# Warp products on finished byte addresses, loaded sixteen at a time; router gates from one tanh

## The reference

```python
# stage 0, cond: rigid transform of each image, bilinear from four neighbours
ix = (gx_n + 1.0) * 0.5 * (w - 1);  iy = (gy_n + 1.0) * 0.5 * (h - 1)
ix0, iy0 = floor(ix), floor(iy);    wx1, wy1 = ix - ix0, iy - iy0
out = gather(iy0i, ix0i) * (wy0 * wx0) + gather(iy0i, ix1i) * (wy0 * wx1)
    + gather(iy1i, ix0i) * (wy1 * wx0) + gather(iy1i, ix1i) * (wy1 * wx1)
# stage 0, ffn: two ternary linear layers with a gelu between (act_quant, weight_quant)
# stage 1, cond: attention pooling within an image (tanh scores, mask, softmax)
# stage 1, ffn: four experts, the best two per row
logits = xf @ wr + br
topk_vals, topk_idx = jax.lax.top_k(logits, 2)
gates = jax.nn.softmax(topk_vals, axis=-1)
out = einsum('nk,nkd->nd', gates, y_sel - c_sel + c_sum)
# stage 2: an adapter with a layer norm, then a frequency-domain product
# stage 3: a linear layer chosen by category, then a gated ternary ffn with a silu
```

## Time and profile before

| | |
|---|---|
| time, 3 runs | 2594.36 us median, 2581.16 to 2600.14 |
| the profiled execution | 2577.68 us, span 2575.9 us |
| granted TensorE clock, mean | 0.912 |
| DVE instructions in the profile | 7954, of them 4096 warp products |

### The profile page before, as it was taken

How to read it: one execution, slowest core, us unless ns; L and a number is a source line. 1 busy time by engine, 2 the same in 40 slices (tenths; PEclk the granted TensorE clock), 3 DMA queues, 4 the chain that set the end, 5 groups by cost and what they waited for, 6 DMA issues and landing times. The chain is left out here.

```text
span 2575.9 us, 50738 instructions
## 1 busy us (share of the span) xinstructions
PE 2090.7 (81%) x12000; PEld 1613.5 (63%) x12000; DVE 1786.6 (69%) x7954; ACT 1647.6 (64%) x2802; POOL 988.1 (38%) x1092
## 2 busy tenths in 40 slices
PE   1334697888888898898898889988888898999975
PEld 1112476666766676676676667766766777777742
DVE  4878777677777777777787778777877564544344
ACT  1035556566777776776777778777666587767542
POOL 1434455545444544344444444454434211221110
PEclk8655799999999999998999999999999999999977
DMA  7344544354545545534455455554554445355531
GB/s 256 110 143 129 170 118 144 112 154 127 149 124 166 150 150 146 175 114 131 141 176 156 137 151 156 169 172 146 142 173 142 125 141 165 122 169 178 158 97 53
DMA packets 306147, 375.94 MB, mean 146 GB/s; under 512 B 127122, under 2 KB 251447, under 8 KB 292924
## 3 DMA queue, kind: packets, MB, share of 16 engines
q1 hardware_dynamic: 274848, 297.02, 37.9%
q0 software_dynamic: 28672, 68.21, 9.4%
q10 hardware_dynamic: 2332, 7.47, 0.7%
HBM read 291.23 MB, written 72.93 MB: 141 GB/s over the span
## 5 line engine op out<-in xcount | busy, mean ns | idle before, releaser
L1177 POOL DMA_INDIRECT w_win<-in_windows,w_idx x512 | 524.0, 1024 | 831.7 <-DMA w_win<-in_windows,w_idx 645.4
L799 DVE TENSOR_TENSOR w_prod<-w_win,w_hat 128x36 f32<-128x36 f32 x4096 | 530.4, 220 | 266.0 <-issue 263.2
L1568 PE MATMUL bank<-moe_w,moe_hidden_T 128*128 x2528 | 644.1, 396 | 18.0 <-DVE moe_y L1010 11.2
L1552 PE MATMUL bank<-moe_xT,moe_w_tile 128*128 128x256 f32 (+1 forms) x3008 | 636.4, 356 | 8.1 <-ACT moe_xT L1337 7.7
L1552 PEld LDWEIGHTS bank<-moe_xT,moe_w_tile 128*128 128x128 f32 x3008 | 513.2, 195 | 84.0 <-ACT moe_xT L1337 14.7
L1568 PEld LDWEIGHTS bank<-moe_w,moe_hidden_T 128*128 128x128 f32 x2528 | 474.5, 197 | 98.2 <-issue 36.5
L1354 ACT ACTIVATE moe_hidden_T<-bank,moe_b 128x256 f32<-128x256 f32 (+1 forms) x752 | 288.6, 436 | 166.0 <-PE bank L1552 139.5
L1354 ACT ACT_TABLE_LOAD x151 | 193.7, 1283 | 71.6 <-PE bank L1552 55.4
L1211 POOL DMA_INDIRECT moe_y_back<-moe_out_sorted,rows_back x128 | 127.7, 998 | 275.6 <-DMA moe_y_back<-moe_out_sorted,rows_back 152.7
L1197 POOL DMA_INDIRECT moe_in_sorted<-c,rows x128 | 138.3, 1080 | 245.1 <-DVE rows L940 104.3
L1096 DVE SCALAR_TENSOR_TENSOR hidden_back<-bank,back_stats,hidden_back 128x512 f32<-128x512 f32 x128 | 95.3, 745 | 107.4 <-ACT hidden_back L1394 105.6
(11 more groups left out here) (260 smaller groups left out, 3749.2 us busy)
## 6 DMA issues: line engine op xcount, KB each, us to landing
moe_w_tile<-in_moe_w SPq DMA_DIRECT2D x94, 1024.0 KB
L_cond_W<-in_L_cond_W SPq DMA_DIRECT2D x128, 256.0 KB
adapters<-in_adapter SPq DMA_DIRECT2D x128, 192.5 KB
gamma_beta<-in_gamma_beta SPq DMA_DIRECT2D x128, 128.0 KB
moe_x<-moe_in_sorted SPq DMA_DIRECT2D x64, 256.0 KB
moe_out_sorted<-moe_y SPq DMA_DIRECT2D x64, 256.0 KB
x_front<-in_x SPq DMA_DIRECT2D x32, 256.0 KB
w_win<-in_windows,w_idx POOLq DMA_INDIRECT x512
```

Source lines behind the costliest of these rows:

```text
L799: ins = v.tensor_tensor(out3, win, hy, ALU.mult)
L1177: gp.indirect_dma_start(out=V[:, g_ * WLEN:(g_ + 1) * WLEN], out_offset=None, in_=t["windows"], in_offset=bass.IndirectOffsetOnAxis(ap=idx ...
L1552: last = te.matmul((H0, H1)[r % 2][:, (f % FPU) * TILE:(f % FPU) * TILE + width(n)], W1[n % 3][:, d * F + f * P:d * F + (f + 1) * P], XT[: ...
L1568: last = te.matmul(Y[:, u * D:(u + 1) * D], hT[:, (f % (2 * FPU)) * TILE + u * P:(f % (2 * FPU)) * TILE + (u + 1) * P], ap(moe2, weight + ...
```

## The change

1. V is allocated first, at the fixed byte address V_AT = 16512 of each partition. `prepare` turns the table of element offsets into finished byte addresses: times 4, plus V_AT, plus the image's place in V (a new column W_AT of the constants). One more small DVE instruction, once.
2. A product's window is given by the register alone, as an access of bytes cast to float32. The register arithmetic per product (multiply, add) has nothing left to compute.
3. The 32 registers of an image are loaded sixteen at a time. The load for k = 0 to 15 is issued in the previous image, directly behind L803's add and ahead of the yield; the load for k = 16 to 31 stands between the second and third batch of products, ahead of the yield there. The wait for a group's offsets (`s_off`) moves with the first load to the end of the previous group.
4. Router: ACT takes Tanh (scale 0.5) instead of Exp; DVE multiplies it by the mask of the second choice (OH + 8) instead of by the mask of both, sums, and two TENSOR_SCALARs on 128x2 write the gates 0.5 - 0.5 s and 0.5 + 0.5 s. The reciprocal, two products and one reduction are gone. Three bare yields keep the places in the order.

```diff
-            ch.link(v.scalar_tensor_tensor(woff[:, :], low[:, 0:PX], float(WY), low[:, PX:2 * PX], ALU.mult, ALU.add))
+            ch.link(v.scalar_tensor_tensor(low[:, 0:PX], low[:, 0:PX], float(WY), low[:, PX:2 * PX], ALU.mult, ALU.add))
+            ch.link(v.tensor_scalar(woff[:, :], low[:, 0:PX], 4.0, wcst[:, W_AT:W_AT + 1], ALU.mult, ALU.add))
...
+            V8 = V.bitcast(U8)
+            def addresses(q, a, j_):
+                par, low_ = q % 2, V_AT + 4 * a * IWIN
+                if a == 0 and j_ == 0:
+                    dve.wait_ge(s_off[par], 8 * (q - par) + 16)
+                first = woff[par][0:1, a * PX + j_ * GI:a * PX + (j_ + 2) * GI]
+                _, at = nc.values_load_multi_w_load_instructions(
+                    first, engines=[mybir.EngineType.DVE], min_val=low_, max_val=low_ + 4 * ((WX - TAP) * WY + WY - TAP),
...
+                return [r.with_bounds(guaranteed_mod_val=0, out_of_modulus=4) - V_AT for r in at]
+            def window(at):
+                return bass.AP(tensor=V8, offset=at, ap=[[4 * QI * IWIN, P], [4 * WLEN, NG], [4 * WY, TAP], [1, 4 * TAP]]).bitcast(F32)
...
+                    if q == 0 and a == 0:
+                        ready[:] = addresses(q, a, 0)
                     dve.wait_ge(s_win[a], 16 * NG * (q + 1))
-                    if a == 0:
-                        dve.wait_ge(s_off[par], 8 * (q - par) + 16)
...
-                    first = woff[par][0:1, a * PX:(a + 1) * PX]
-                    _, shift = nc.values_load_multi_w_load_instructions(
...
                         if k and k % GI == 0:
+                            if k % (2 * GI) == 0:
+                                ready[:] = addresses(q, a, k // GI)
                             yield
-                        win = ap(V, shift[k] + a * IWIN, [[WLEN, NG], [WY, TAP], [1, TAP]])
+                        win = window(ready[k % (2 * GI)])
...
-                    yield from ch.spaced(v.tensor_tensor(col, row(0), row(1), ALU.add))
+                    add = v.tensor_tensor(col, row(0), row(1), ALU.add)
+                    add.then_inc(ch.sem, 1)
...
+                    if a + 1 < QI or q + 1 < NQ:
+                        ready[:] = addresses(q + (a + 1) // QI, (a + 1) % QI, 0)
+                    yield
+                    dve.wait_ge(ch.sem, step)
...
-                ins = v.tensor_tensor(lg[:, EX:EX + 8], lg[:, EX:EX + 8], lg[:, SL:SL + 8], ALU.mult)
+                ins = v.tensor_tensor(lg[:, EX:EX + 8], lg[:, EX:EX + 8], lg[:, OH + 8:OH + 16], ALU.mult)
...
-                yield from ch.spaced(v.reciprocal(lg[:, SE:SE + TT], lg[:, SE:SE + TT]))
-                ins = v.tensor_tensor(ap(lg, GA, [[EXP, TT], [1, EXP]]), e3, ap(lg, SE, [[1, TT], [0, EXP]]), ALU.mult)
-                yield from ch.spaced(ins)
+                g0 = q * 2 * TT
+                v.tensor_scalar(GP[:, g0:g0 + TT], lg[:, SE:SE + TT], -0.5, 0.5, ALU.mult, ALU.add)
+                v.tensor_scalar(GP[:, g0 + TT:g0 + 2 * TT], lg[:, SE:SE + TT], 0.5, 0.5, ALU.mult,
+                                ALU.add).then_inc(E["m_gat"], 1)
...
-                yield from ch.spaced(v.tensor_tensor(prod, slot2, both(GA), ALU.mult))
-                v.tensor_reduce(GP[:, bass.ds(q * 2 * TT, 2 * TT)], ap(lg, PR, [[EXP, 2 * TT], [1, EXP]]), AX.X,
-                                ALU.add).then_inc(E["m_gat"], 1)
+                yield
+                yield
+                yield
...
-                s.activation(lg[:, 82:90], lg[:, 0:8], ACT.Exp).then_inc(E["a_lge"], 1)
+                s.activation(lg[:, 82:90], lg[:, 0:8], ACT.Tanh, scale=0.5).then_inc(E["a_lge"], 1)
```

More of the change, by code:

```diff
@@ L15 @@
 I32 = mybir.dt.int32
+U8 = mybir.dt.uint8
 ALU = mybir.AluOpType
@@ L75 @@
 WLEN = WX * WY
+V_AT = 16512
 MKW = P + 1
@@ L79 @@
 QPX = QI * IPX
-W_GX, W_GY, W_IV, W_JV, W_BASE = 0, NG, NG + 1, NG + 1 + GI, NG + 1 + GI + GJ
+W_GX, W_GY, W_IV, W_JV, W_AT, W_BASE = 0, NG, NG + 1, NG + 1 + GI, NG + 1 + GI + GJ, NG + 2 + GI + GJ
 WCONST = W_BASE + B
@@ L257, in sem @@
             return ctx.enter_context(nc.semaphore(name))
+        V = sb("w_win", QI * IWIN)
         cst = sb("const", CCONST)
@@ L432, in _ @@
             ch.link(v.tensor_scalar(low[:, :], low[:, :], MAGIC, 0.0, ALU.subtract, ALU.max))
-            v.tensor_tensor(fd[:, :], fd[:, :], low[:, :], ALU.subtract)
-            ch.link(v.scalar_tensor_tensor(woff[:, :], low[:, 0:PX], float(WY), low[:, PX:2 * PX], ALU.mult, ALU.add))
+            ch.link(v.tensor_tensor(fd[:, :], fd[:, :], low[:, :], ALU.subtract))
+            ch.link(v.scalar_tensor_tensor(low[:, 0:PX], low[:, 0:PX], float(WY), low[:, PX:2 * PX], ALU.mult, ALU.add))
+            ch.link(v.tensor_scalar(woff[:, :], low[:, 0:PX], 4.0, wcst[:, W_AT:W_AT + 1], ALU.mult, ALU.add))
             dve.sem_inc(s_geo, 1)
@@ L440, in network @@
         ("cst", "idb", "wq", "wmean", "moe2", "moeb1", "router", "brB"))
-    b1B, b2B, fbB, attW, attb, attv, freqM, KB, ones, ids, nhalf, hmag, frD, fdD, idxD, offD, XS, YS, XMD = (g[k] for k in
+    b1B, b2B, fbB, attW, attb, attv, freqM, KB, ones, ids, nhalf, hmag, frD, fdD, idxD, offD, XS, YS, XMD, V = (g[k] for k in
         ("b1B", "b2B", "fbB", "attW", "attb", "attv", "freqM", "KB", "ones", "ids", "nhalf", "hmag", "frD", "fdD", "idxD",
-         "offD", "XS", "YS", "XMD"))
+         "offD", "XS", "YS", "XMD", "V"))
     s_raw, s_ld = g["s_raw"], g["s_ld"]
@@ L777, in coords @@
                 ins.then_inc(E["t"], 1)
+            V8 = V.bitcast(U8)
[6 more added lines that the diff above has]
+                    first, engines=[mybir.EngineType.DVE], min_val=low_, max_val=low_ + 4 * ((WX - TAP) * WY + WY - TAP),
+                    skip_runtime_bounds_check_because="the shift inside a group is bounded by its shape for any angle")
+                return [r.with_bounds(guaranteed_mod_val=0, out_of_modulus=4) - V_AT for r in at]
+            def window(at):
+                return bass.AP(tensor=V8, offset=at, ap=[[4 * QI * IWIN, P], [4 * WLEN, NG], [4 * WY, TAP], [1, 4 * TAP]]).bitcast(F32)
+            ready = []
             def warp(q):
@@ L783, in warp @@
                     yield
+                    if q == 0 and a == 0:
+                        ready[:] = addresses(q, a, 0)
                     dve.wait_ge(s_win[a], 16 * NG * (q + 1))
-                    if a == 0:
-                        dve.wait_ge(s_off[par], 8 * (q - par) + 16)
                     if a % 2 == 0:
                         dve.wait_ge(E["hat"], 2 * q + a // 2 + 1)
-                    first = woff[par][0:1, a * PX:(a + 1) * PX]
-                    _, shift = nc.values_load_multi_w_load_instructions(
-                        first, engines=[mybir.EngineType.DVE], min_val=0, max_val=(WX - TAP) * WY + WY - TAP,
-                        skip_runtime_bounds_check_because="the shift inside a group is bounded by its shape for any angle")
                     for k in range(PX):
                         if k and k % GI == 0:
+                            if k % (2 * GI) == 0:
+                                ready[:] = addresses(q, a, k // GI)
                             yield
-                        win = ap(V, shift[k] + a * IWIN, [[WLEN, NG], [WY, TAP], [1, TAP]])
+                        win = window(ready[k % (2 * GI)])
                         hy = ap(H, HY + (a * PX + k) * NG, [[1, NG], [0, TAP], [QPX, TAP]])
@@ L802, in warp @@
                     row = lambda k: ap(M, k * IPX * TAP, [[IPX, TAP], [1, IPX]])
-                    yield from ch.spaced(v.tensor_tensor(col, row(0), row(1), ALU.add))
+                    add = v.tensor_tensor(col, row(0), row(1), ALU.add)
+                    add.then_inc(ch.sem, 1)
+                    ch.n += 1
+                    step = ch.base + ch.n
+                    if a + 1 < QI or q + 1 < NQ:
+                        ready[:] = addresses(q + (a + 1) // QI, (a + 1) % QI, 0)
+                    yield
+                    dve.wait_ge(ch.sem, step)
                     yield from ch.spaced(v.tensor_tensor(col, col, row(2), ALU.add))
@@ L1740 @@
     wc[:, W_JV:W_JV + GJ] = np.arange(GJ)
+    wc[:, W_AT] = V_AT + 4 * IWIN * (p % QI)
     wc[:, W_BASE:] = (np.arange(B)[None, :] * PYW - YLO) * PXR - XLO
```

1 line of the change is left out of this document (removed).

## The result

| | before | after |
|---|---|---|
| time, 20 runs each | 2584.85 us median | 2575.47 us median |
| the profiled execution | 2577.68 us, span 2575.9 | 2571.66 us, span 2569.9 |

The ratio is 0.9953 (95% interval 0.9937 to 0.9970): 12 us less, where the prediction had 71.

What follows compares the result with a forecast made beforehand. DVE was taken to bound the first 2022 us, PE close behind. Savings of 40 + 40 + 5 = 85 us on DVE, 0.8 of them arriving (68), plus 3 from ACT gave 71 us less: 2523 us, range 2462 to 2577.

Steps and rivals of the forecast that it cites:

- A load of 16 values: 1.18 us: DVE's register load: 16 values cost 1.18 us, on a straight line between one value (0.310) and 32 (2.105).
- register operations pace half of the batches: DVE's products: the sequencer paces some batches at 130 ns a product; without register operations all run at 107, 40 us less.
- Idle of 0.73 and 0.80 us behind the two loads: DVE per image: the first load leaves 0.73 us idle, the second 0.80; with 0.11 for a break, 1.64 against 1.95.
- the lead that eight products can win (0.27 us): Before the second load: eight products without register operations win DVE's sequencer 0.27 us of lead over the engine.
- rival 1: More gain: the sequencer is nearly always ahead, loads hide, DVE gains some 185 us, 130 arrive, about 2465 us; chance 0.13.
- The term "40 us" for the load: DVE's register loads: splitting and placing them saves 0.31 us an image, 40 us over 128 images.
- Router 5 us on DVE, 3 us at the end: Router: two fewer small DVE instructions per group save 5 us; ACT's saved table loads count 3 us at the end.
- 0.8 of DVE's gain reaches the end: Whole kernel: 0.8 of the 85 us saved on DVE, 68 us, shortens the total time.
- DVE's busy time, issue and waits for POOL together as 95%: Between 300 and 2000 us: 1307 + 207 + 96 = 1610 of 1700 us, leaving DVE's queue almost no slack.
- POOL as running ahead of DVE: Between 300 and 2000 us: POOL waits 71 us for DVE to give the window back, so it runs ahead.
- rival 2: Gain absorbed: DVE waits for POOL, whose fixed part is above 80%; two thirds of 85 us go, about 2570; chance 0.12.
- Wrong if DVE's waits for POOL grow by more than some 20 us: Sign in the changed kernel's profile: growth of DVE's waits for POOL beyond some 20 us would show the forecast wrong.

Runs made afterwards that it cites:

- e16: Changed kernel with gathers not waiting for each other and register arithmetic kept on every product, fourth chip: 0.9976 of the kernel before.
- e18: Kernel before with the router's tanh change alone, gathers still waiting, fourth chip: 0.9999 of the kernel before.
- e8: Changed kernel with gathers not waiting for each other, but one load of 32 addresses at the image's head: 0.9401 of the kernel before.
- e7: Changed kernel with gathers not waiting for each other, plus an unused 1.21 us DVE reduction per image: 0.9502 of the kernel before.

## Why the prediction was wrong

- *A load of 16 values: 1.18 us.* 1.10, right; so was the reading that register operations pace half of the batches (495 us, as forecast; 477 of 512 batches of eight now take under 1 us, where 259 did).
- *Idle of 0.73 and 0.80 us behind the two loads.* Wrong: inside the loads DVE idles 0.35 and 0.02 us. I gave the sequencer the lead that eight products can win (0.27 us) and no more, and held against rival 1 that the waits before every batch and add take the lead away. Without its register operations it keeps a lead over other threads' instructions too, ten instructions or 1.2 us at the most; with them it has 0.56 us of idle in the same place (e16). The term "40 us" for the load, over the whole span, measured 167 us (225 to 58). That was the mechanism of rival 1, which I gave 0.13.
- *Router 5 us on DVE, 3 us at the end.* The counts are right (26 reloads fewer at the gelus, 32 at the router); at the end nothing that e18 can see.
- *0.8 of DVE's gain reaches the end.* This is the step that decided, and it failed. With a larger gain than forecast (167 us in loads and 35 in products over the whole span, against 80) the time fell by 12, 0.06 of it. I took DVE's busy time, issue and waits for POOL together as 95% and called the bound DVE; the 96 us of waits for POOL belonged to the other side, and they grew by 98 us. And I read POOL as running ahead of DVE from its 71 us of waits for the window, without adding up the rest of its queue, which comes to 91% of the stretch in its own pace. I had 514 and 74 us of landing waits in front of me and left out 61 us of further landing waits and 120 us of issue in the same queue; so I wrote "above 80%" under rival 2.
- *Rival 2, at 2570 us with a chance of 0.12,* is what happened, for its reason. That its number fits is luck: it lets two thirds of 85 us go, where over nine tenths of 202 us went.
- *Wrong if DVE's waits for POOL grow by more than some 20 us.* They grew by 98.

What stays open: the measured slopes don't add up to the result. At 0.15 to 0.36 per microsecond of DVE, 202 us would be 30 to 73 us and not 12. Idle time inside a load may be worth less than engine work (0.17 from e8 to e1, where e7 has 0.36 for work in the same kernel), perhaps because a good part of it would have been a wait for another engine anyway; no run separates that.

## What to carry to other kernels

Before costing a gain on one engine, add up each other engine's queue in the same stretch as busy + waits for its own DMAs + issue. Here the queue that reached 91% that way held the kernel back although its busy share was 46%, and the waits of DVE for its results grew by 98 us, over half of what DVE saved in the stretch. A queue of indirect DMAs that wait for each other's landing is worth a try: here freeing it was worth 7% together with this change on a chip where the change alone gave 0.5%, 3% on another, and nothing there without the change. And compare versions on one chip, side by side: the same edit gave 0.954 and 1.004 on two.

## What the runs showed of the hardware

- A register load takes 0.31 us for one value, 1.10 us for 16 and 2.10 us for 32: 53 ns per value up to 16, 63 ns from 16 to 32.
- DVE's sequencer got up to ten instructions ahead, 6.5 started in the mean during a 1.10 us load between batches, and the load cost the engine 0.02 us. With a 57 ns register operation per product (e16) 3.5 started, and it cost 0.56 us.
- An indirect DMA costs POOL 1.25 us in its queue if it waits for nothing. If it waits for the landing of the one before, it starts 3.5 us behind it (median of after, 2.8 to 5.6 for eight in ten).
- In traces from two of the four chips short sequencer instructions take 0.4 to 1.4 us in places. On the fourth a kernel with free gathers takes 115 to 142 us more than on the first, the kernel before 11.
- None of the router's 32 Tanh had a table load in front of it; the last table loaded before it was in 27 of them that of a Gelu and in 5 that of the Silu.
